# A fused block with one adapter per sequence: each pair's two adapters computed alone instead of all eight under a mask

## What is computed

```python
H = jnp.einsum('btd,od->bto', x, W)
A_b = A[adapter_idx]
B_b = Bm[adapter_idx]
s_b = scalings[adapter_idx]
xa = jnp.einsum('btd,brd->btr', x, A_b)
delta = jnp.einsum('btr,bor->bto', xa, B_b)
delta = jax.lax.stop_gradient(delta * s_b[:, None, None])
return H + delta
```

## Time and profile before

| | us |
|---|---|
| median of 3 runs | 994.13 (992.5 to 996.27) |
| profiled execution, own time | 993.04 |
| its span, first to last instruction | 991.2 |
| TensorE busy in the span | 938.0 (95%) |
| DVE, ACT, POOL busy | 600.8, 385.4, 514.6 |

### The profile page before, as it was taken

One profiled execution on the slowest core, in us unless ns is written; L12 is line 12 of the kernel. 1 busy time (PEld: TensorE's weight loads), 2 busy tenths in 40 slices (PEclk: granted clock), 3 DMA queues, 4 the chain that ended last, 5 costly groups with the idle time before them and its releaser, 6 DMA issues.

```text
span 991.2 us, 22128 instructions
## 1 busy us (share of the span) xinstructions
PE 938.0 (95%) x6253; PEld 679.9 (69%) x6253; DVE 600.8 (61%) x1788; ACT 385.4 (39%) x1061; POOL 514.6 (52%) x469
## 2 busy tenths in 40 slices
PE   6899999999999999999976999999899999899997
PEld 4576766766766767667665777777677777677775
DVE  5334434656656544357554767777677677676775
ACT  2122121221221221222225656565565656565653
POOL 1345555355464477653565555555455555555530
PEclk9999999999999999999999999999999999999999
DMA  9779887777668767687456565656565666556641
GB/s 313 267 255 314 299 276 267 242 236 272 237 231 274 232 239 263 216 279 258 151 183 177 155 194 165 196 175 191 155 189 181 182 199 198 168 176 195 199 134 45
DMA packets 105162, 212.48 MB, mean 214 GB/s; under 512 B 29563, under 2 KB 52056, under 8 KB 96930
## 3 DMA queue, kind: packets, MB, share of 16 engines
q1 hardware_dynamic: 71042, 145.54, 43.4%
q0 software_dynamic: 25088, 57.74, 19.7%
q10 hardware_dynamic: 8992, 8.73, 2.8%
HBM read 204.39 MB, written 33.86 MB: 240 GB/s over the span
## 4 chain that ended last, share of the span: by engine, by line
PE 90%; issue 2%; DVE 2%; another core or an unknown queue 2%; ACT 2%; DMA 1%; SPq 1%; ACTq 0%; DVEq 0%
PE banks L589 11%; PE banks L755 10%; PE banks L803 10%; PE banks L707 9%; PE banks L791 7%; PE banks L628 6%; PE banks L636 6%; PE banks L638 6%; PE banks L778 4%; PE banks L732 3%; PE banks L839 3%; PE banks L697 3%; PE banks L712 3%; PE banks L796 2%; PE banks L599 2%
## 5 line engine op out<-in xcount | busy, mean ns | idle before, releaser
L548 POOL DMA_INDIRECT ring<-new_rows,idx x128 | 131.0, 1023 | 86.5 <-DVE big L1280 31.0
L460 POOL TENSOR_TENSOR rms<-ss,neg_half 128x12 f32<-128x12 f32 x31 | 70.9, 2286 | 180.7 <-DVE ss L1185 180.7
L931 ACT ACTIVATE big<-big,neg_max 128x320 f32<-128x320 f32 x256 | 141.5, 555 | 3.1 <-DVE neg_max L1243 2.5
L1243 DVE CUSTOM_DVE_ANT_0 big<-banks,mask 128x320 f32<-128x320 f32 x256 | 114.6, 485 | 14.6 <-PE banks L755 10.8
L755 PE MATMUL banks<-kt,q_in 64*128 64x192 f32 (+2 forms) x768 | 103.0, 366 | 20.0 <-remote 10.6
L589 PE MATMUL banks<-ring 128*64 128x512 f32 x512 | 117.1, 599 | 3.1 <-DMA ring<-in_w 3.1
L872 ACT ACTIVATE x2t_hi<-banks 128x512 fp32r<-128x512 f32 x32 | 19.1, 598 | 235.6 <-PE banks L599 235.6
L755 PEld LDWEIGHTS banks<-kt,q_in 64*128 64x128 f32 x768 | 78.8, 188 | 43.2 <-remote 14.1
L501 POOL DMA_INDIRECT ring<-in_kvrows,idx x64 | 61.2, 957 | 60.5 <-PE banks L755 42.8
L921 ACT ACTIVATE kt<-banks 128x384 f32<-128x384 f32 x128 | 61.9, 484 | 74.1 <-PE banks L733 52.6
L589 PEld LDWEIGHTS banks<-ring 128*64 128x64 f32 x512 | 33.9, 136 | 81.5 <-issue 79.4
(11 more groups left out here) (169 smaller groups left out, 2011.6 us busy)
## 6 DMA issues: line engine op xcount, KB each, us to landing
ring<-in_w SPq DMA_DIRECT2D x62, 1024.0 KB, 5.9
ring<-in_xt SPq DMA_DIRECT2D x32, 256.0 KB
x_in<-in_x SPq DMA_DIRECT2D x32, 256.0 KB, 5.5
bias_in<-in_b SPq DMA_DIRECT2D x64, 128.0 KB, 5.4
x_dram<-x SPq DMA_DIRECT2D x32, 256.0 KB, 4.9
q_dram<-q_t ACTq DMA_DIRECT2D x32, 256.0 KB
new_rows<-kv_out SPq DMA_DIRECT2D x32, 256.0 KB, 4.7
q_in<-q_dram SPq DMA_DIRECT2D x64, 128.0 KB
```

The source lines that it names most:

```text
L548: pool.indirect_dma_start(out=kv[:, s, c, :], out_offset=None, in_=new_rows, in_offset=bass.IndirectOffsetOnAxis(ap=idx[:, b, 1 + c:2 + c] ...
L931: nc.scalar.activation(prob[:, s % 2, PLACE[g] * NK:(PLACE[g] + 1) * NK], sm[:, s % 2, g, :], ACT.Exp, bias=neg_max[:, s % 2, g:g + 1], sc ...
L1243: V.tensor_tensor_reduce(sm[:, s % 2, g, :], ps_s[g], mask[:, s % 2, k0:k0 + NK], 1.0, 3.0e38, ALU.add, ALU.min, accum_out=neg_max[:, s % ...
```

## The change

The host gives the second matrices three times over (3 x 16 rows per adapter), the scalings as one column per adapter, and the adapter numbers in the small table of indices. Per pair, ACT reads each sequence's adapter number, starts a transfer of its 48 x 512 second matrix into `pair_b`, and copies its first matrix, scaled and repeated three times, into a tile of 64 columns of `pair_a` (rows 48 to 63 are zero). TensorE makes the first product in two column tiles of 64, one for each sequence, with only the tokens of that sequence. ACT rounds the result (`xa_hi`) and DVE makes `xa_parts`: high, high and low part stacked in rows. ACT and DVE make `pair_b_parts` in the same way (high, low, high). The second product is then a single rounded product. From pair 2 on the first product stands inside `project_inputs`, between the query and the key/value columns. The first product's wait for the mask becomes a wait for `xa_ready`.

Before the loop ACT takes the adapters of pairs 0 and 1 and rounds those of pair 0, and DVE splits those of pair 0. In step k, ACT rounds pair k + 1's and takes pair k + 2's at the end; DVE splits pair k + 1's behind the sum x2. POOL zeroes `pair_b` and the padding of `pair_a` at the start. `lora_b`, its load and the mask's preparation are gone.

```diff
                 sp.dma_start(lora_a[:, :, :], a["la"]).then_inc(ld_la, 16)
-                sp.dma_start(lora_b[:, :], a["lb"]).then_inc(ld_lb, 16)
...
+            nc.gpsimd.memset(pair_b[:, :, :], 0.0).then_inc(pb_set, 1)
+            nc.gpsimd.memset(pair_a[:, :, :, :, ROLE_ROWS:], 0.0).then_inc(pb_set, 1)
...
+            def adapt_down(k, s):
+                pe.wait_ge(pa_ready, k + 1)
+                pe.wait_ge(x1t_ready, k + 1)
+                wait(pe, xa_ready, k)
+                if isinstance(k, int) and k == NP - 1:
+                    pe.wait_ge(idx_ready, 1)
+                for c in range(DC):
+                    for h in range(2):
+                        last = nc.tensor.matmul(ps_la[T * h:T * h + T, 0:T], pair_a[:, s, h, c, :], x1t[:, c, T * h:T * h + T],
+                                                start=(c == 0), stop=(c == DC - 1))
+                last.then_inc(la_done, 1)
...
                     for ps_out, n0 in ((ps_q, 0), (ps_kv, D)):
+                        if n0 == D and on(k, 0, NP) and not (isinstance(k, int) and k == 1):
+                            adapt_down(k, s)
...
-                    for c in range(DC):
-                        last = nc.tensor.matmul(ps_la[:, 0:P], lora_a[:, c, :], x1t[:, c, :], start=(c == 0), stop=(c == DC - 1))
-                    last.then_inc(la_done, 1)
+                    if isinstance(k, int) and k < 2:
+                        adapt_down(k, s)
...
-                    nc.tensor.matmul(ps_l1[:, :], xam[:, s, :], lora_b[:, :], start=False, stop=True).then_inc(h_done, 1)
+                    pe.wait_ge(xa_ready, k + 1)
+                    pe.wait_ge(pb_ready, k + 1)
+                    nc.tensor.matmul(ps_l1[:, :], xa_parts[:, :], pair_b_parts[:, :], start=False, stop=True).then_inc(h_done, 1)
...
+            def take_adapters(k, s):
+                for h in range(2):
+                    n = act.value_load(ids_sb[0:1, 3, bass.ds(k * 2 + h, 1)], min_val=0, max_val=NA - 1)
+                    act.dma_start(pair_b[T * h:T * h + ROLE_ROWS, s, :], a["lb"][bass.ds(n, 1)].rearrange("o q d -> (o q) d")).then_inc(
+                        ld_pb[s], 16)
+                    last = nc.scalar.activation(
+                        pair_a[:, s, h, :, 0:ROLE_ROWS].rearrange("p c (q r) -> p c q r", r=RANK),
+                        lora_a[:, :, bass.ds(n * RANK, RANK)].unsqueeze(2).to_broadcast([P, DC, ROLES, RANK]), ACT.Copy,
+                        scale=scaling[:, bass.ds(n, 1)])
+                last.then_inc(pa_ready, 1)
+            def round_adapters(k, j, s):
+                act.wait_ge(ld_pb[s], 2 * 16 * (j + 1))
+                wait(act, pb_ready, k)
+                nc.scalar.activation(pair_b_hi[:, :], pair_b[:, s, :], ACT.Copy).then_inc(pb_hi_ready, 1)
+            act.wait_ge(ld_ids, 16)
+            act.wait_ge(ld_small, 2 * 16)
+            act.wait_ge(pb_set, 2)
+            act.wait_ge(ld_la, 16)
+            for k in range(2):
+                take_adapters(k, k)
+            round_adapters(0, 0, 0)
...
+                if on(k, 0, NP):
+                    act.wait_ge(la_done, k + 1)
+                    wait(act, xa_ready, k)
+                    nc.scalar.activation(xa_hi[:, :], ps_la[:, 0:T], ACT.Copy).then_inc(xa_hi_ready, 1)
...
+                if on(k, -1, NP):
+                    round_adapters(k + 1, j + s, 1 - s)
+                if on(k, -2, NP):
+                    take_adapters(k + 2, s)
...
+            def split_adapters(k, s):
+                dve.wait_ge(pb_hi_ready, k + 1)
+                wait(dve, h_done, k)
+                V.scalar_tensor_tensor(pair_b_parts[:, :], pair_b_hi[:, :].bitcast(F32), fcols[:, BPART:BPART + 1], pair_b[:, s, :],
+                                       ALU.mult, ALU.add).then_inc(pb_ready, 1)
...
-                    V.tensor_tensor(xam[:, s, :].rearrange("p (h t) -> p h t", h=2), ps_la[:, 0:P].rearrange("p (h t) -> p h t", h=2),
-                                    lora_mask[:, bass.ds(k * 2, 2)].unsqueeze(2).to_broadcast([P, 2, T]), ALU.mult).then_inc(xam_ready, 1)
+                    for h in range(2):
+                        t0, t1 = T * h, T * h + T
+                        last = V.scalar_tensor_tensor(xa_parts[t0:t1, t0:t1], xa_hi[t0:t1, :].bitcast(F32), fcols[t0:t1, ACOL:ACOL + 1],
+                                                      ps_la[t0:t1, 0:T], ALU.mult, ALU.add)
+                    last.then_inc(xa_ready, 1)
...
+                if on(k, -1, NP):
+                    split_adapters(k + 1, r)
+            split_adapters(0, 0)
             loop(dve, phase_one, 2, 4, NP + 2, PREP_STEP)
```

More of the change, by code:

```diff
@@ L34 @@
 EPS = 1e-6
+ROLES = 3
+ROLE_ROWS = ROLES * RANK
 NONE = 60000
@@ L82, in build @@
         gain_in = reals[:, REAL_COLS[4]:].rearrange("p (w d) -> p w d", w=2)
-        numbers = sb("numbers", [P, 1 + 2 * NB], I32)
-        own_len, kvl_row, ad_row = numbers[:, 0:1], numbers[:, 1:1 + NB], numbers[:, 1 + NB:]
-        ids_sb = sb("ids_sb", [1, 3, NB], I32)
-        lora_mask = sb("lora_mask", [P, NB])
+        numbers = sb("numbers", [P, 1 + NB], I32)
+        own_len, kvl_row = numbers[:, 0:1], numbers[:, 1:]
+        ids_sb = sb("ids_sb", [1, 4, NB], I32)
         neg_half = sb("neg_half", [P, 12])
@@ L150, in build @@
             lora_a = sb("lora_a", [P, DC, P], F32, first)
-            lora_b = sb("lora_b", [P, D], F32, first)
+            pair_a = sb("pair_a", [P, 2, 2, DC, T], F32, first)
+            pair_b = sb("pair_b", [P, 2, D], F32, first)
+            pair_b_hi, pair_b_parts = (sb(n, [P, D], F32R, first) for n in ("pair_b_hi", "pair_b_parts"))
+            xa_hi = sb("xa_hi", [P, T], F32R, first)
+            xa_parts = sb("xa_parts", [P, P], F32R, first)
             x1t = sb("x1t", [P, DC, P], F32, first)
@@ L197, in build @@
         t2_done, qkv_done, t3_done = sem("t2_done"), sem("qkv_done"), sem("t3_done")
-        x1_ready, xam_ready, x2_ready = sem("x1_ready"), sem("xam_ready"), sem("x2_ready")
+        x1_ready, x2_ready = sem("x1_ready"), sem("x2_ready")
+        ld_pb = [sem(f"ld_pb{i}") for i in range(2)]
+        pa_ready, pb_hi_ready, pb_ready, pb_set = sem("pa_ready"), sem("pb_hi_ready"), sem("pb_ready"), sem("pb_set")
+        xa_hi_ready, xa_ready = sem("xa_hi_ready"), sem("xa_ready")
         ss_ready, ab_ready = sem("ss_ready"), sem("ab_ready")
@@ L655, in phase_one @@
                     transpose_x2(k, r)
-                    project_inputs(k)
+                    project_inputs(k, s)
                     experts(k, j, s)
@@ L665, in phase_one @@
                     pe.wait_ge(rows_ready, 1)
[L666 removed]
+                    pe.wait_ge(xa_ready, NP - 1)
                     for c in range(2):
@@ L688, in phase_one @@
                 if on(k, 0, NP):
-                    pe.wait_ge(x1t_ready, k + 1)
-                    wait(pe, xam_ready, k)
-                    if isinstance(k, int) and k == NP - 1:
-                        pe.wait_ge(idx_ready, 1)
-                    if isinstance(k, int) and k == 0:
-                        pe.wait_ge(ld_la, 16)
-                    for c in range(DC):
-                        last = nc.tensor.matmul(ps_la[:, 0:P], lora_a[:, c, :], x1t[:, c, :], start=(c == 0), stop=(c == DC - 1))
-                    last.then_inc(la_done, 1)
+                    if isinstance(k, int) and k < 2:
+                        adapt_down(k, s)
                     wait(pe, x2_ready, k)
@@ L1169, in phase_one @@
                 if on(k, 0, NP):
-                    dve.wait_ge(la_done, k + 1)
-                    wait(dve, h_done, k - 1)
-                    V.tensor_tensor(xam[:, s, :].rearrange("p (h t) -> p h t", h=2), ps_la[:, 0:P].rearrange("p (h t) -> p h t", h=2),
-                                    lora_mask[:, bass.ds(k * 2, 2)].unsqueeze(2).to_broadcast([P, 2, T]), ALU.mult).then_inc(xam_ready, 1)
+                    dve.wait_ge(xa_hi_ready, k + 1)
+                    wait(dve, h_done, k)
+                    for h in range(2):
+                        t0, t1 = T * h, T * h + T
+                        last = V.scalar_tensor_tensor(xa_parts[t0:t1, t0:t1], xa_hi[t0:t1, :].bitcast(F32), fcols[t0:t1, ACOL:ACOL + 1],
+                                                      ps_la[t0:t1, 0:T], ALU.mult, ALU.add)
+                    last.then_inc(xa_ready, 1)
                 if isinstance(k, int) and k == 0:
@@ L1332 @@
     fcols[:, 0] = T * b + 1
-    fcols[:, 1] = row // RANK
+    fcols[:, 1] = np.where(row % T // RANK == 2, -1.0, 0.0)
+    fcols[:, 7] = np.where(row % T // RANK == 1, -1.0, 0.0)
     fcols[:, 2] = b * NWIN
```

30 lines of the change are left out of this document (12 added, 18 removed).

## The result

| | before | after |
|---|---|---|
| median of 4 runs | 994.75 us | 1046.15 us |
| lowest to highest | 992.5 to 996.27 | 1042.07 to 1047.65 |
| ratio, 95% interval | | 1.0502 (1.047 to 1.0533) |
| profiled execution, its time / span | 993.04 / 991.2 us | 1046.26 / 1044.5 us |
| query transposes in steps 2, 3 and 31 (start, us) | 51.85, 66.93, 490.84 | 67.14, 84.70, 541.66 |

The kernel became 5% slower. The forecast was 1028 us, the range 1008 to 1044: the direction and the mechanism were right, the amount was not, and the time lies 2 us above the range.

What follows compares the result with a forecast made beforehand. TensorE was taken as the bound, with a chain through ACT, DVE and POOL hidden by 0.17 us that would then rule. 29 periods x 0.88 = +25.5, start +10, end -1: 1027.5, so 1028 us; range 1008 to 1044.

Steps and rivals of the forecast that it cites:

- the chain: From the projections' end through ACT, DVE and POOL to the query transposes: 8.37 us beside TensorE's 8.54, hidden by 0.17.
- The period: Phase one's time per pair: 7.18 + 8.37 + 0.05 = 15.60 us, with 0.45 for the port 16.05, against 15.17 before.
- the moved product: First adapter product, now ahead of the last eight projection products: 0.55 us (0.41 to 1.03) added in front of the chain.
- the port: DVE's split of the second matrices meets POOL's rotation sum; the scaled queries grow 0.45 us a pair (bounds 0 and 0.69).
- my 6.63: TensorE's stretch in the kernel before, from the query transposes' weight load to the projections' end, in us.
- The second product: Second adapter product, one rounded product: 0.95 us becomes 0.33, a gain of 0.62 a pair in the stretch beside the chain.
- I take +10 us: Start, ACT's work before the loop: first x1 12 us later, some 3 back, about 1.5 lost again; +5 to +14.
- 192 KB more per pair, due two steps later: The loop's added transfers of second matrices; no time was put into the sum for them.
- End -1: After the last pair's projections, the exposed old path shrinks by 0.62 + 0.81: about -2 us, counted as -1.
- The first (the port doesn't hurt): Rival: DVE's split finds a gap, period 15.60 us, +21.5 us, 1015 us; chance 0.14.
- The second, TensorE as the bound: Rival: TensorE's own 14.29 us period rules if the chain is below 7.1 us; 976.5 us, faster; chance 0.09.
- The third: Rival: exposed weight loads or a late ACT, or the port's full 0.69; 1042 to 1049 us; chance 0.15.

Runs made afterwards that it cites:

- b_no_second: The kernel before without its second adapter product, so without the adapter's part of the result: ratio 0.9965.
- b_queries_first: The kernel before, with POOL summing and scaling queries ahead of keys and the query transposes waiting for the queries alone: ratio 0.9969.
- a_product_behind: The changed kernel with the first adapter product, for pairs from 2 on, replaced by sixteen products of its size behind the projections: ratio 1.0317.
- a_split_early: The changed kernel with DVE's split of the second matrices moved from behind the sum x2 to between x2t_lo and x1t_lo: ratio 1.0422.
- the lazy start: The changed kernel with reads and loads of pairs 0 and 1 issued at once and pair 0's copies, rounding and split behind its x1t: ratio 1.0352.
- a_no_pair_loads: The changed kernel without the second matrices' loads from pair 2 on; those of pairs 0 and 1 are reused: ratio 1.0444.
- a_table_first: The changed kernel with only POOL's rotation table put ahead of the next pair's sum of x and bias: ratio 1.0421.
- a_all_four: The changed kernel with queries first on POOL, the lazy start, the early split and the table first: ratio 0.9961.
- a_all_five: a_all_four with ACT's store of the queries issued behind the squares and the value copy: ratio 0.9899 against the kernel before.

## Why the prediction was right or wrong

**What bounds it: right.** TensorE had idled nowhere, and the chain was hidden by 0.17 us. b_no_second and b_queries_first shorten one side each, by 0.95 and 1.2 us a pair, and both gain 0.3 to 0.4%.

**The period: right, from terms that were each somewhat off.** I took 0.55 for the moved product and 0.45 for the port. The product is 0.62, and the four products behind it pay 0.12 more for a weight load that no longer overlaps; a_product_behind prices the move at 0.84. What hid the 0.12 is that my 6.63 began with a weight load 0.11 ahead of the first product, which a waiting TensorE doesn't have. By the Trainium skill's rule on row groups (TensorE: Matmul & The Clock Gate, What overlaps and what doesn't) the sum had gone to the upper end, 1.03; the trace speaks for covered loads among the sixteen. The meeting of DVE and POOL costs the chain 0.33 to 0.34 (a_split_early). As in the earlier trace rows the two take turns: the split starts beside POOL's rotation sum, ends 0.55 us behind that sum's end at 211.70, and takes 2.06 in all in place of 0.75 to 0.84; POOL's scaled queries, which start at 211.78, take 1.37 in place of 1.04. The Trainium skill's rule of a port held for the whole instruction (SBUF — State Buffer, SBUF: two separate sides) would have given 0.69. The trace agrees with the taking of turns, and not with that size. 7.25 + 8.72 + 0.12 = 16.09 against my 16.05.

**The second product: right.** It has 0.32 to the experts' start, forecast 0.33, and it earned nothing, as the forecast said.

**"I take +10 us" for the start: the first step that failed.** By step 2's query transposes it is 15.3 us. Two errors in it cancelled: I let ACT begin at 19.19, the end of w1's rounding, but that rounding now starts at 19.17 in place of 17.28 and ends at 21.08; and the four reads and copies take 4.3 us from there, not 6.8, so the last copy ends at 25.34 (forecast 26.0). The rounding of w1 waits for its load; it starts at 16.9 to 18.2 in the four traces with the old adapter and at 18.5 to 20.1 in the ten with the new one. The reason was not looked for.

Three terms did not cancel. Pair 0's loads, issued at 20.82 and 22.05, landed by 29.2 in place of 27, so the first x1 is 14.4 us late, not 12. The "some 3 us" that I let come back did so only for a while: pair 0's second adapter product ends at 38.73 (27.48 before), 11.3 us later. But then the sum x2 waits for DVE, which works on the projection weights' low part (L1207, 3.09 us) until 40.75, and starts at 40.78, 13.3 us later than in the earlier trace rows. And the clock fell. The projections that start next take 8.0 us to the experts (43.31 to 51.34) where they took 5.7 (29.61 to 35.31), the first eight of them 3.78 in place of 2.14. Granted clock (the third column from the end) while TensorE did nothing, from 18 to 31 us, and beside those products:

```profile
18.00:31.00 13.00, 0.00 (x0) 0.00 (x0) 1.11 (x2) 4.35 (x6) 0.00 (x0) 0.62 1.07 329
42.00:48.00 6.00, 5.31 (x14) 3.95 (x14) 3.45 (x3) 0.60 (x1) 0.01 (x1) 0.50 0.86 297
```

The same for the kernel before, where it runs these products:

```profile
28.00:34.00 6.00, 5.04 (x23) 4.04 (x24) 3.10 (x3) 0.60 (x1) 0.52 (x1) 1.00 0.57 188
```

0.50 is the 1.2 GHz level, 1.00 that of 2.4 GHz. The idle 13 us do not stand directly before the second fall: between 35 and 41 us the clock was 1.00 again, and just before it fell at 41.6 TensorE had been idle for 2.80 us (38.73 to 41.53), waiting for that sum x2. In the lazy start, where that wait is 0.78 us, the same eight products take 2.14. I wrote that I put no fall of the clock into the sum, and argued from phase two, where it stays at 1.00.

**"192 KB more per pair, due two steps later", costed at nothing: the second step that failed.** The 29 periods were to bring 25.5 us and brought 35.5. My 15.17 was a single pair; the 29 periods of the kernel before average 15.14, which makes 29 x 0.91 = 26.4 of the forecast. The first period (17.6) is 1.5 over: its x1 transposes wait for DVE's x1, which follows POOL's bias sum of 67.02. The nine lengthened ones are 7.1 over, and some 0.5 is spread over the others. The second matrices themselves are in time. But their loads make the others later, and these stand in a loop of their own that I had not drawn. Medians from issue to landing of the bias, for the kernel before, after, and a_no_pair_loads: 5.4, 6.6 and 6.2. That most of the growth remains without the loads is not explained. That loop and added loads together are the cause of seven of the nine is shown twice: without the loads, and with them but the table first, these go. Their worth is 3 to 5 us of the 10 (the 28 periods fall by 3.3 us in a_no_pair_loads and 5.1 in a_table_first); the two beside the indirect transfers and the first period stay.

**"End -1": wrong by 3.5.** The stretch behind step 31's query transposes grew by 2.5 us. 0.7 of it lies ahead of the last query transposes, in the two steps where I expected a gain. 1.8 lies in phase two, in which nothing was edited. The 14 traces of this case have 475.7 to 481.3 us there, so this may be no effect of the change; no experiment decides it.

Together: start 5.3 more than forecast, the loop 10, the end 3.5. That is 18.8, and 34.5 + 18.8 = 53.3.

**The rivals.** The first (the port doesn't hurt) falls with 1.38 us for the scaled queries. The second, TensorE as the bound, falls: it waits 48.6 us. It did decide in a_all_four and a_all_five, once the chain was some 1.5 us shorter (1.2 by the queries first, 0.33 by the early split): periods of 14.6, where 14.29 was its own work by my sum. The third reached the right time for a wrong reason: it has exposed loads of weights and a late ACT, while the products take 0.62 us and x2t_hi waits for TensorE alone. None of my terms stood for a loop that I had not looked for.

## What to carry to other kernels

When TensorE shows no idle time, find the loops that lie just behind it, from each engine's wait back to itself one iteration later, the queues and their loads included, and write down the period of each; an edit pays only by the distance to the second longest. Here the same change costs 5%, and with five reorderings that add no work it gains 1% (two of them alone gain 0.3% in the kernel before). Preparation put ahead of the loop was paid in full here, and once more where TensorE waited and its clock fell; taken out of the way it gave back only what the next wait, for the experts' matrices, left.

## What the runs showed of the hardware

- Sixteen products of 64 weight columns by 64 streamed ones take 0.62 us, 0.04 each, all with the same 128 rows. The trace draws their weight loads in the same stretch, 0.55 us for sixteen; what is not covered is the first load of the next group of full 128 x 128 ones, 0.12 us: it starts with that group's first product (219.09), where the next group's starts 0.23 ahead of its own (219.89 for 220.12).
- A DVE operation with two inputs of 128 x 512 in on-chip memory takes 0.75 to 0.84 us alone. Started 0.30 behind POOL's sum of 1.81 us it takes 2.06, ending 0.55 behind the sum, and POOL's next operation, already begun, takes 0.33 more.
- ACT's transfer issued while POOL issues indirect transfers is followed by ACT's next operation 0.5 to 2.1 us late in the four pairs where the two meet. With the transfer moved behind the squares, two of the four pairs recover. So the transfer's place is at most one cause of the delay.
- A number read, the issue of a transfer and a scaled copy of 128 x 192 on ACT repeat every 1.2 us (from 21.35 to 24.89 for three steps), in place of my 1.7.
